# Block scales of x and h from one scalar_tensor_tensor over a strip of floors, in a fused linear attention and FP4 feed-forward block

## What is computed

```
def fp4_quant_dequant(x):
    xb = x.reshape(shape[:-1] + (shape[-1] // BLOCK, BLOCK))
    scale = jnp.max(jnp.abs(xb), axis=-1, keepdims=True) / 6.0
    scale = jnp.maximum(scale, jnp.float32(1e-12))
    xn = xb / scale
    idx = jnp.searchsorted(_MID, jnp.abs(xn))
    q = _GRID[idx] * jnp.sign(xn) * scale
gate = fp4_linear(x, w_gate)
y = fp4_linear(x, w_up)
h = jax.nn.silu(gate) * y
return fp4_linear(h, w_down)
```

## Time and profile before

| what | value |
|---|---|
| median of 3 runs | 1361.32 us (1359.19 to 1363.07) |
| the profiled execution, its time | 1361.72 us |
| the profiled execution, its span | 1360.0 us |
| DVE busy | 1309.7 us, 96% |
| PE busy | 1271.1 us, 93% |
| ACT busy | 969.4 us, 71% |
| POOL busy | 355.0 us, 26% |
| DMA queues, share of 16 engines | 46.8% on q1 |
| chain that ended last | DVE 52%, issue 33%, DVEq 7%, PE 5% |

### The profile page before, as it was taken

The page is one execution under the profiler, slowest core; times in us unless marked ns, Lnnn a source line. Parts: engine busy times, 40 slices in busy tenths (PEclk is TensorE's granted clock), DMA queues, the critical chain, the costliest instruction groups (busy, mean ns, idle before and its releaser), DMA issues.

```text
span 1360.0 us, 41012 instructions
## 1 busy us (share of the span) xinstructions
PE 1271.1 (93%) x9934; PEld 871.0 (64%) x9934; DVE 1309.7 (96%) x3901; ACT 969.4 (71%) x3221; POOL 355.0 (26%) x791
## 2 busy tenths in 40 slices
PE   0279999999999999999999999999999999999996
PEld 0157666666666666666666666666666666666664
DVE  6869999999999999999999999999999999999996
ACT  1567777777777777777777777777777777777772
POOL 2212223222222323222222222223232222323220
PEclk9889999999999999999999999999999999999998
DMA  4024544444454444444544444545454454445444
GB/s 129 12 40 82 108 98 100 105 100 102 98 114 100 101 105 98 103 100 98 113 101 105 98 102 99 112 98 104 105 109 99 92 115 101 96 105 110 97 83 91
DMA packets 432380, 133.64 MB, mean 98 GB/s; under 512 B 397404, under 2 KB 431836, under 8 KB 432348
## 3 DMA queue, kind: packets, MB, share of 16 engines
q1 hardware_dynamic: 431622, 132.60, 46.8%
q10 hardware_dynamic: 726, 0.72, 0.2%
HBM read 19.99 MB, written 16.78 MB: 27 GB/s over the span
## 4 chain that ended last, share of the span: by engine, by line
DVE 52%; issue 33%; DVEq 7%; PE 5%; ACT 2%; DMA 1%; SPq 0%; ACTq 0%
DVE hx_v L880 7%; DVE ga L810 5%; DVE blk L834 3%; DVE xring L963 3%; DVE hx_v L887 3%; DVE h L820 2%; DVE drec L794 2%; DVE xq_s L935 2%; DVE q_rows L922 2%; DVE att L799 2%; DVE osum L958 2%; DVE blk L843 1%; DVE dz L786 1%; DVE hrow L854 1%; DVE dmx L790 1%
## 5 line engine op out<-in xcount | busy, mean ns | idle before, releaser
L418 POOL TENSOR_TENSOR xn_s<-xn,xn_s 128x256 f16<-128x256 f32 x128 | 108.6, 848 | 820.3 <-ACT xn_s L535 820.3
L1165 PE MATMUL outp<-w_down_cat,q_rows 128*128 128x256 f16 x1408 | 246.1, 274 | 0.0
L617 ACT ACTIVATE snap<-ctxp,mask 64x68 f32<-64x68 f32 x1024 | 236.5, 310 | 3.3
L1165 PEld LDWEIGHTS outp<-w_down_cat,q_rows 128*128 128x128 f16 x1408 | 138.3, 98 | 16.5
L1167 PE MATMUL outp<-w_down_lo,q_rows 128*128 128x256 f16 x640 | 147.6, 274 | 0.0
L580 ACT ACTIVATE th<-unit0a,c_g 128x352 f32<-128x352 f32 x128 | 71.0, 554 | 97.3 <-PE unit0b L1078 95.3
L556 ACT ACTIVATE qexp<-qsh,c_q 128x256 f32<-128x256 f32 x128 | 65.1, 508 | 99.0 <-DVE qsh L773 98.8
L580 ACT ACTIVATE th<-unit1a,c_g 128x352 f32<-128x352 f32 x128 | 71.0, 555 | 87.4 <-PE unit1b L1078 65.0
L827 DVE TENSOR_REDUCE blk<-h 128x44 f32<-128x704 f32 x128 | 123.8, 967 | 0.1
L411 POOL TENSOR_TENSOR att_s<-att,att_s 128x256 f16<-128x256 f32 x128 | 87.9, 687 | 108.1 <-ACT att_s L572 108.1
L880 DVE TENSOR_TENSOR hx_v<-h,blk 128x704 f32<-128x704 f32 x128 | 111.0, 868 | 0.0
(11 more groups left out here) (199 smaller groups left out, 4059.0 us busy)
## 6 DMA issues: line engine op xcount, KB each, us to landing
xring<-x SPq DMA_DIRECT2D x128, 128.0 KB, 2.7
out<-xring SPq DMA_DIRECT2D x128, 128.0 KB, 2.5
xnt<-xn_s SPq DMA_TRANSPOSE x128, 2.5
xqt<-xq_s SPq DMA_TRANSPOSE x128, 2.4
att_t<-att_s SPq DMA_TRANSPOSE x128, 2.5
q_rows<-q_rows SPq DMA_TRANSPOSE x128, 3.6
raw_qkv<-wqkv_t SPq DMA_DIRECT2D x1, 768.0 KB, 4.4
raw_up<-wup ACTq DMA_DIRECT2D x2, 352.0 KB
```

Of the source, the lines that this page charges most:

```text
L418: nc.gpsimd.tensor_tensor(xn_s[:, par, 1, :], xn[:, par, :], xn_s[:, par, 0, :], ALU.subtract).then_inc(xn_lo, 1)
L617: nc.scalar.activation(kept[:, :, cols], sums[:, :, cols], ACT.Copy, scale=mask[rows, f, h:h + 1])\
L1165: nc.tensor.matmul(downp, hqt[:, par, m, :], w_down_cat[:, m, :], start=(m == 0), stop=False)
```

## The change

The two tensor_scalar instructions of `block_scales` become one scalar_tensor_tensor over all 60 block maxima: multiply by the constant, then max with a second tensor, `blk_floor`, a strip of 60 fp32 for each partition. The strip is filled once at the start by a memset (16 columns, the floor of x) and a copy of `h_floor` spread over 44 columns. A new semaphore `blk_scaled` counts the combined step; `xq_step` now has 5 counts for each tile and `hq_step` 8, so every wait on them is renumbered. In the first three steps (x alone) and the last three (h alone) the instruction covers just its part. The whole diff, but for waits that are only renumbered:

```diff
+        blk_floor = sb("blk_floor", [P, FB + XB])
...
+        blk_scaled = sem("blk_scaled")
...
             def scales_x(t):
-                act.wait_ge(xq_step, after(t, 6, 2))
+                act.wait_ge(blk_scaled, t + 1)
...
             def block_scales(t, u):
-                if is_tile(u):
-                    dve.wait_ge(xq_step, after(u, 6, 1))
-                    nc.vector.tensor_scalar(xblk[:, 1, :], xblk[:, 0, :], SIX_TIE * 2.0 ** 11, XS * TINY * 2.0 ** 11, ALU.mult, ALU.max)\
-                        .then_inc(xq_step, 1)
-                if is_tile(t):
-                    dve.wait_ge(hq_step, after(t, 9, 1))
-                    nc.vector.tensor_scalar(hblk[:, 1, :], hblk[:, 0, :], SIX_TIE * 2.0 ** 11, h_floor[:, :], ALU.mult, ALU.max)\
-                        .then_inc(hq_step, 1)
+                do_h, do_x = is_tile(t), is_tile(u)
+                if do_h:
+                    dve.wait_ge(hq_step, after(t, 8, 1))
+                if do_x:
+                    dve.wait_ge(xq_step, after(u, 5, 1))
+                if do_h or do_x:
+                    both = slice(0 if do_h else FB, FB + XB if do_x else FB)
+                    nc.vector.scalar_tensor_tensor(blk[:, 1, both], blk[:, 0, both], SIX_TIE * 2.0 ** 11, blk_floor[:, both],
+                                                   ALU.mult, ALU.max).then_inc(blk_scaled, 1)
 
             def over_one(t, u):
                 do_h, do_x = is_tile(t), is_tile(u)
                 if do_h:
-                    dve.wait_ge(hq_step, after(t, 9, 2))
+                    dve.wait_ge(blk_scaled, t + 4)
                     nc.vector.tensor_reduce(hrow[:, 0, :], hblk[:, 1, :], AX.X, ALU.max).then_inc(hq_step, 1)
                 if do_h or do_x:
                     if do_x:
-                        dve.wait_ge(xq_step, after(u, 6, 2))
+                        dve.wait_ge(blk_scaled, u + 1)
                     both = slice(0 if do_h else FB, FB + XB if do_x else FB)
                     nc.vector.reciprocal(blk[:, 2, both], blk[:, 1, both]).then_inc(hx_step, 1)
...
             nc.vector.tensor_scalar(h_floor[:, :], h_floor[:, :], 2.0 * TINY * 2.0 ** 11, None, ALU.mult).then_inc(factors, 1)
+            nc.vector.memset(blk_floor[:, FB:FB + XB], XS * TINY * 2.0 ** 11).then_inc(factors, 1)
+            dve.wait_ge(factors, 12)
+            nc.vector.tensor_copy(blk_floor[:, 0:FB], h_floor[:, :].broadcast_to([P, FB])).then_inc(factors, 1)
...
-            dve.wait_ge(factors, 11)
+            dve.wait_ge(factors, 13)
```

More of the change, by code:

```diff
@@ L295, in turn_xq @@
                     return
-                sp.wait_ge(xq_step, after(t, 6))
+                sp.wait_ge(xq_step, after(t, 5))
                 sp.sem_inc(sp_turn, 1)
@@ L306, in turn_h @@
                     return
-                sp.wait_ge(hq_step, after(t, 9))
+                sp.wait_ge(hq_step, after(t, 8))
                 sp.sem_inc(sp_turn, 1)
@@ L520, in normalise_waits @@
                 if begun(t - 2):
-                    act.wait_ge(xq_step, after(t - 2, 6, 3))
+                    act.wait_ge(xq_step, after(t - 2, 5, 2))
             def normalise(n, d):
@@ L592, in factor_of_row @@
                     return
-                act.wait_ge(hq_step, after(t, 9, 4))
+                act.wait_ge(hq_step, after(t, 8, 3))
                 if begun(t - 2):
@@ L600, in scales_h @@
                     return
-                act.wait_ge(hq_step, after(t, 9, 5))
+                act.wait_ge(hq_step, after(t, 8, 4))
                 nc.scalar.activation(hs_hi[:, :].rearrange("p (b i) -> p b i", i=2), twice(hblk[:, 1, :]), ACT.Copy,
@@ L818, in times_up @@
                 if begun(t - 2):
-                    dve.wait_ge(hq_step, after(t - 2, 9, 6))
+                    dve.wait_ge(hq_step, after(t - 2, 8, 5))
                 nc.vector.tensor_tensor(h[:, par, half * FH:(half + 1) * FH], ga[:, half, :],
@@ L862, in row_scale @@
                 if is_tile(t):
-                    dve.wait_ge(hq_step, after(t, 9, 3))
+                    dve.wait_ge(hq_step, after(t, 8, 2))
                     if begun(t - 1):
@@ L871, in over_row @@
                     return
-                dve.wait_ge(hq_step, after(t, 9, 4))
+                dve.wait_ge(hq_step, after(t, 8, 3))
                 nc.vector.reciprocal(hrow[:, 2, :], hrow[:, 1, :]).then_inc(hq_step, 1)
@@ L897, in round_hx @@
                     if do_h:
-                        dve.wait_ge(hq_step, after(t, 9, 6))
+                        dve.wait_ge(hq_step, after(t, 8, 5))
                     if do_x:
-                        dve.wait_ge(xq_step, after(u, 6, 3))
+                        dve.wait_ge(xq_step, after(u, 5, 2))
                     nc.vector.tensor_scalar(hx_u[:, both], hx_v[:, both].bitcast(bf16)[:, 1:2 * (both.stop - both.start):2],
@@ L905, in round_hx @@
                     if begun(t - 1):
-                        dve.wait_ge(hq_step, after(t - 1, 9))
+                        dve.wait_ge(hq_step, after(t - 1, 8))
                     if begun(u - 1):
-                        dve.wait_ge(xq_step, after(u - 1, 6))
+                        dve.wait_ge(xq_step, after(u - 1, 5))
                     nc.vector.tensor_scalar(hx_q[:, both], hx_u[:, both].bitcast(u16), GRID16, -GRID16, ALU.add, ALU.add)\
@@ L920, in scale_h @@
                 else:
-                    dve.wait_ge(hq_step, after(t, 9, 7))
+                    dve.wait_ge(hq_step, after(t, 8, 6))
                 nc.vector.tensor_tensor(rows(hq_s[:, par, part * F:(part + 1) * F]), rows(hx_q[:, 0:F].bitcast(fp16)),
@@ L929, in scale_x @@
                 dve.wait_ge(hx_step, hx_after(t, 3))
-                dve.wait_ge(xq_step, after(t, 6, 4))
+                dve.wait_ge(xq_step, after(t, 5, 3))
                 if begun(t - 2):
```

## The result

| what | before | after |
|---|---|---|
| median | 1360.84 us (6 runs) | 1385.20 us (1384.32 to 1386.06, 6 runs) |
| ratio | | 1.0177, 95% interval 1.0165 to 1.0189 |
| the profiled execution's span | 1360.0 us | 1384.1 us |

The change makes the kernel 1.8% slower, 24.4 us. The forecast was 1359.7 us, the range ended at 1366: it was wrong.

The account below looks back on a forecast made before the run. DVE was taken to bound the kernel, PE following closely. From 1361.72 us, less 1.9 for the pairs of steps and plus 0.3 at the start, came 1360.1, as a median 1359.7 us; range 1345 to 1366.

Parts of the forecast that it names:

- rival A: The combined instruction escapes POOL's stop: 28 us faster, 1333 us, or 1350 to 1357 if partial; chance 20%, a third full.
- the two prices weighed: Combined instruction's unstopped duration: 213 ns at 1.02 ns a column over a base of 152, or 0.24 us at 1.4.
- So it starts 0.12 after the old L843 start: Combined instruction waits for h's maximum, ending 0.09 us after L843's old start, and starts 0.04 after that end.
- The sum: Whole forecast: 1.9 us gained over 62 pairs of steps, 0.3 us lost at the start, from 1361.72 to 1360.1 us.
- The lock of L413 onto the even steps: POOL's subtraction (L411 before the change) starts 0.08 us ahead of the combined instruction in even steps and stops it.
- s: Time from L843's old start to L764's start on DVE: forecast 0.70 us in even steps, 0.25 in odd.
- what one step gives the next takes back: The odd step gains 0.06 us, the even step loses 0.03 in its stop; 0.03 us a pair remains.
- single escapes: Steps where the combined instruction avoids POOL's stop: held not to last, the odd step then stopped for some 0.35 us.
- Rival B: The stopped combined instruction starts afresh after POOL's end, 0.30 us rather than 0.07: 12 us slower, 1373 us; chance 13%.
- The added copy and memset at the start: Filling the strip on a full DVE at the start: 0.15 us each, 0.3 us in all, between nothing and 0.6.

Follow-up runs that it names:

- e6: The changed kernel with its two waits swapped, plus three more matmuls of zeros where PE clears the running sums; 1334.23 us, ratio 0.9782.
- e7: The changed kernel with its two waits swapped, and ACT's high_att moved behind kexp so POOL's attention subtraction starts later; 1333.77 us, ratio 0.9781.
- e1: The changed kernel with the two waits ahead of the combined instruction swapped, xq_step first and hq_step second; 1352.16 us, ratio 0.9936.
- e3: The changed kernel with ACT's copy_qt ahead of high_xn, so POOL's subtraction for xn starts later; 1357.83 us, ratio 0.9978.
- e9: The changed kernel, wait order kept, with three more matmuls of zeros where PE clears the running sums; 1358.15 us, ratio 0.9968.

## Why the prediction was wrong

- **What bounds the kernel: right.** DVE, with PE 0.2 us a step behind it. Once the stops are gone PE bounds, at 9.68 us a step and 1334 us (e6, e7), where rival A had 1333.
- **The instruction's duration: right.** 0.21 forecast, 0.22 measured. Of the two prices weighed, the lower one holds: 60 columns at L887's 1.02 ns over the base of 152 give 213 ns. The Trainium skill (Vector Engine (DVE) Microarchitecture Reference, Points that are easy to get wrong) has half the throughput for two SBUF sources that are not bf16. By that the instruction would take about 0.27 us, an estimate from that page over L887's row; the trace does not agree, with 0.22 at the median of 108.
- **"So it starts 0.12 after the old L843 start": this step failed.** The 0.04 us came from L887 to L901, where `hq_step` is waited for first and the wait that blocks, for `xq_step`, second. The changed kernel waits for `hq_step` first and `xq_step` second too, but at L850 it is `hq_step` that blocks; in the loop the first of the two is handled apart and the rest of the issue stands behind it. The gap is 0.136 us in the mean (17.0 us over 125), 0.13 and 0.15 in turn in the loop. Outside the loop, where the counts are constants, the same code starts L850 0.04 after L829's end:

```profile
97.47 0.96 DVE L829 TENSOR_REDUCE blk<-h 128x44 f32<-128x704 f32 x1
98.47 0.22 DVE L850 SCALAR_TENSOR_TENSOR blk<-blk,blk_floor 128x60 f32<-128x60 f32 x1
```

  The diff shows the order of the two waits, and I did not ask which of them blocks, nor which of them stands apart: e1 shows that this differs inside and outside the loop.
- **The sum with that price put in would still have said no change,** since 0.1 us a step is taken up by L413's stop: e3 and e9 have it and stand at 1357.8 and 1358.2 us. The second failure is what the sum left out, and no rival named it: POOL's other two-input subtraction against L922. Both rows stood in the text. L922 started 0.03 us ahead of L418 in the locked step, and 0.09 behind it, at 0.96 us, in another. I used them to learn who stops whom and did not take 0.03 us as a margin that any lateness of DVE might use up. The lateness of 0.1 us does not use it up by itself: from about 200 us until the first boundary L420 of the changed kernel starts 0.12 and 0.29 us behind L925 in turn. The short step of PE at a boundary does, in the kernel before as well, and the wait keeps DVE from getting free again. What it came to is 35.4 us on L925, a term that the sum had at nothing; with it the account gives 25 us, and 24.4 were measured.
- **The lock of L413 onto the even steps: right, where the kernel is in it.** In the later part of e1 s is 0.25 and 0.70 to 0.71 us, as worked out. The statement that what one step gives the next takes back is borne out by e3 and e9.
- **Rival A: right in mechanism and size, and wrong in what brings it.** I let single escapes fall back within a step or two. In e1 the start leaves DVE ahead of PE and the stretch without a stop lasts 28 steps in the loop, until PE's short step at the boundary ends it.
- **Rival B: wrong.** L850's end is 0.08 us after L413's, in e1 as in the early steps of the changed kernel, never a whole instruction. The slow result came by another road.
- **The added copy and memset at the start: right.** The trace of the changed kernel has the memset with 0.07 us and the copy with 0.19, 0.26 together against 0.3 forecast. What they cost the whole kernel no run separates.

What remains open: how much later DVE must be for the state to hold itself. L922 of the kernel before takes 0.96 to 1.00 us at 391.78, in the four steps from 708.99 to 739.50, and at 1026.40, at the three boundaries, and gets free after one step, four and one. In the four steps POOL's lead over L922 goes 0.093, 0.073, 0.054, 0.094 us, and in the fifth, at 0.037, it is POOL that is stopped. They are 10.17 us apart in the mean, against 10.22 in the changed kernel, which fits a state that just fails to hold; but no run varied the delay in small steps to find the point.

## What to carry to other kernels

When an instruction needs several semaphores, see in the trace which of the waits is made apart from it, and put one there that is met long before, so that the instruction itself carries the one that blocks. In this loop that means the blocking wait last, and the order of two waits is worth 33 us; outside the loop it means the blocking wait first. In a kernel where two engines are within 3% of each other, a sum over one engine's instructions is not enough: list each pair of instructions that can stop one another, with its margin in the trace, and ask which margins a change of 0.1 us, or one step of another engine that is shorter than the rest, uses up. And if a stop follows another engine's clock, look for the move that separates the two instructions (here one activation moved on ACT, 26 us in the kernel before) before shortening anything.

## What the runs showed of the hardware that was not expected

- Two waits ahead of one instruction, the first of them blocking, leave 0.13 to 0.15 us of idle time in the loop, against 0.035 with the order turned (e1). Outside the loop, with constant counts, it is the other way round: 0.035 with the blocking wait first, 0.105 with it last.
- A DVE instruction that reads two tensors from SBUF and a POOL instruction that does so run one after the other. Which goes first was settled by less than 0.1 us: with POOL 0.09 ahead DVE lost 0.44 us, with POOL 0.03 behind POOL lost 0.34, and in the kernel before POOL was stopped even when it started 0.06 ahead (401.90 us). A program with such a pair can have several steady states: the changed kernel's pairs of steps take 20.4 us in one, e3's 19.75, e6's 19.36, and a single PE step shorter by 0.34 us decides which it falls into. The changed kernel itself runs at 19.75 us a pair from about 200 us until the first boundary.
- More matmuls made the kernel faster (e6 against e1, 18 us), by keeping engines in step.
